# Relative-position attention and a gated FFN: the order of SyncE's scratch transfers, 8 KB rows for queries and keys, and a smaller first block

## The reference, cut to what matters

```python
Q, K, V = (x @ W.T).reshape(b, s, H, HD).transpose(0, 2, 1, 3)      # for each of Wq, Wk, Wv
idx = clip(r[None, :] - r[:, None], -256, 256) + 256
scores = (einsum('bhqd,bhkd->bhqk', Q, K) + einsum('bhqd,qkd->bhqk', Q, pek[idx])) / SCALE
attn = softmax(where(causal, scores, -inf))
out = einsum('bhqk,bhkd->bhqd', attn, V) + einsum('bhqk,qkd->bhqd', attn, pev[idx])
x = layernorm(x + out @ Wo.T)
x = layernorm(x + (silu(x @ wg.T) * (x @ wu.T)) @ wd.T)             # wg, wu, wd = integers / 127
```

## Time and profile before

| | |
|---|---|
| median of 3 runs | 6102.4 us (6099.91 to 6109.79) |
| the profiled execution, whole | 6102.18 us |
| its span in the trace | 6100.5 us |
| busy, share of the span | PE 86%, DVE 63%, ACT 56%, POOL 32% |
| moved by DMA | 1488.37 MB, mean 244 GB/s |

### The profile page before, as it was taken

How to read it: one execution, slowest core, us unless ns; L and a number is a source line. 1 busy time by engine, 2 the same in 40 slices (tenths; PEclk the granted TensorE clock), 3 DMA queues, 4 the chain that set the end, 5 groups by cost and what they waited for, 6 DMA issues and landing times. The chain is left out here.

```text
span 6100.5 us, 143149 instructions
## 1 busy us (share of the span) xinstructions
PE 5228.9 (86%) x49460; PEld 3460.5 (57%) x49460; DVE 3820.3 (63%) x8777; ACT 3442.9 (56%) x7512; POOL 1936.5 (32%) x2580
## 2 busy tenths in 40 slices
PE   9968888888888888888888888888888889999999
PEld 5645555555555555555555555555555546556665
DVE  5646666666666666666667666666666645555554
ACT  4546767667666667767667666766667611111111
POOL 4443333333333333333333333333333311111111
PEclk9989999999999999999999999999999989999999
DMA  8989999999999999999999999999989821121111
GB/s 247 281 228 296 299 290 296 297 292 298 296 289 293 292 297 305 295 295 296 289 300 301 297 293 295 299 292 290 298 276 302 282 77 55 57 64 58 55 55 38
DMA packets 694267, 1488.37 MB, mean 244 GB/s; under 512 B 68132, under 2 KB 365704, under 8 KB 693640
## 3 DMA queue, kind: packets, MB, share of 16 engines
q1 hardware_dynamic: 693640, 1480.16, 76.9%
HBM read 775.21 MB, written 704.65 MB: 243 GB/s over the span
## 5 line engine op out<-in xcount | busy, mean ns | idle before, releaser
L746 ACT ACTIVATE a_prob<-a_neg_s,a_neg_max 128x384 f32<-128x384 f32 (+2 forms) x2048 | 1177.6, 575 | 188.9 <-DVE a_neg_max L795 168.3
L717 PE MATMUL a_t_ps<-a_ident,a_band 128*128 128x128 f32 x3840 | 646.3, 290 | 579.9 <-DMA a_band<-prob_scr 565.3
L478 DVE COPY a_p_t<-a_t_ps 128x512 f32<-128x512 f32 (+3 forms) x1536 | 954.7, 622 | 281.3 <-PE a_t_ps L710 274.4
L753 ACT ACTIVATE a_b_out<-a_t_ps 128x512 f32<-128x512 f32 (+1 forms) x1024 | 583.0, 570 | 904.9 <-PE a_t_ps L653 903.1
L643 PE MATMUL a_s_ps<-a_k,a_q 96*128 96x512 bf16 (+3 forms) x3072 | 880.8, 342 | 140.8 <-ACT a_far L750 127.8
L710 PE MATMUL a_t_ps<-a_ident,a_prob 128*128 128x128 f32 x5376 | 949.1, 279 | 0.4 <-DVE a_band_t L484 0.2
L795 DVE CUSTOM_DVE_ANT_1 a_neg_s<-a_s_ps,a_bias,a_far_neg 128x384 f32<-128x384 f32 x1280 | 791.1, 618 | 237.2 <-DVE a_far_neg L789 237.2
L671 PE MATMUL a_o_ps<-a_p_t,a_v 128*32 128x128 f32 x18432 | 862.9, 303 | 0.2 <-ACT a_o_t L758 0.2
L789 DVE TENSOR_REDUCE a_far_neg<-a_s_ps 128x1 f32<-128x640 f32 (+4 forms) x1280 | 709.9, 555 | 218.1 <-PE a_s_ps L643 165.1
L717 PEld LDWEIGHTS a_t_ps<-a_ident,a_band 128*128 128x128 f32 x3840 | 440.5, 147 | 713.1 <-issue 525.3
L753 ACT ACTIVATE a_p_t<-a_t_ps 128x512 f32<-128x512 f32 (+3 forms) x1536 | 669.1, 436 | 157.8 <-PE a_t_ps L710 152.0
(11 more groups left out here) (97 smaller groups left out, 6551.8 us busy)
## 6 DMA issues: line engine op xcount, KB each, us to landing
a_bias<-bias_scr SPq DMA_DIRECT2D x512, 576.0 KB, 5.5
bias_scr<-a_b_out SPq DMA_DIRECT2D x512, 512.0 KB, 6.6
a_band<-prob_scr SPq DMA_DIRECT2D x512, 512.0 KB, 6.5
prob_scr<-a_prob SPq DMA_DIRECT2D x448, 576.0 KB, 7.2
qk_scr<-p_parts SPq DMA_DIRECT2D x128, 384.0 KB, 3.2
a_q<-qk_scr SPq DMA_DIRECT2D x384, 128.0 KB, 5.2
a_k<-qk_scr SPq DMA_DIRECT2D x384, 128.0 KB, 5.9
prob_scr<-a_wide SPq DMA_DIRECT2D x64, 576.0 KB, 6.6
```

What stands on the lines that cost most here:

```text
L478: copy(p_t[par][:, u, blocks[0] * P:(blocks[-1] + 1) * P], bank[:, 0:len(blocks) * P]) \
L717: mm = pe.transpose(bank[:, n * P:(n + 1) * P], band[:, kk % 2, 2 * i + n // 2, (n % 2) * P:(n % 2 + 1) * P], ident[:, :])
L746: e = act.activation(near_prob(k, u, near(qb)), neg_s[:, u % 2, 0:w].rearrange("p (b c) -> p b c", c=P), ACT.Exp, bias=neg_max[:, u:u + 1] ...
L753: read_out(act, lambda o, i: act.activation(o, i, ACT.Copy), "act", r, k, u, first, last)
```

## The change

Three things, and what they bring with them.

1. On SP the bias write of tile k+3 stands ahead of the bias read of tile k+2; before it stood behind the loads.
2. Queries and keys are stored so that four heads of one feature lie side by side: the columns of Wq and Wk are permuted when ACT copies them (line 190), a row of `qk_scr` for one part and feature holds 4 x 1024 tokens (8 KB), and the terms are put in the orders (0, 1, 2, 0, 1, 0) and (2, 1, 0, 1, 0, 0), so that runs of three, two and one parts can be loaded as one DMA each (`RUNS`): six loads of a group where there were twelve, in steps 0 to 3; v comes in step 4. The key parts are stored in reversed order. The projection writes each m with two DMAs of 64 partitions.
3. In the first query block only the half that exists is moved, packed to rows of 512 elements (`run_of`), both ways; ACT writes its probabilities straight to `wide0`, and POOL has nothing to add there.

The rows of `bias_scr` get a pitch of 1152 elements (`WIDE`) with zero padding behind each, where they had 1024.

```diff
-TERMS_Q = (0, 0, 1, 1, 0, 2)
-TERMS_K = (0, 1, 0, 1, 2, 0)
+TERMS_Q = (0, 1, 2, 0, 1, 0)
+TERMS_K = (2, 1, 0, 1, 0, 0)
+RUNS = ((0, 3, 0), (3, 2, 0), (5, 1, 0)), ((0, 3, 0), (3, 2, 1), (5, 1, 2))
...
-                        sp.dma_start(qk_scr[m // 2, r * 2 + m % 2, :, :, j * CHUNK:(j + 1) * CHUNK]
-                                     .rearrange("s p t -> p s t"), parts[:, m]).then_inc(part_saved[m], 16)
+                        for g in range(2):
+                            sp.dma_start(qk_scr[m // 2, r * 2 + m % 2, g, :, :, j * CHUNK:(j + 1) * CHUNK]
+                                         .rearrange("s p t -> p s t"), parts[g * P // 2:(g + 1) * P // 2, m]) \
+                                .then_inc(part_saved[m], 16)
...
-                act.activation(w_t[:, n // 2, n % 2], tr_ps[:, n % 2, 0:dim], ACT.Copy).then_inc(w_ready, 1)
+                dst, src = w_t[:, n // 2, n % 2], tr_ps[:, n % 2, 0:dim]
+                if n < 4:
+                    dst = dst.rearrange("p (g d h) -> p g h d", d=HD, h=GRP)
+                    src = src.rearrange("p (g h d) -> p g h d", d=HD, h=GRP)
+                act.activation(dst, src, ACT.Copy).then_inc(w_ready, 1)
...
-        LOADS = 2
+        LOADS = ((0, 0),), ((1, 0),), ((0, 1), (0, 2)), ((1, 1), (1, 2))
...
+        def run_of(qb):
+
+            return ROW if qb else GRP * P
...
+            def load_qk(r, g, some=((0, 0), (1, 0), (0, 1), (0, 2), (1, 1), (1, 2))):
+                for which, n in some:
+                    first, count, at = RUNS[which][n]
+                    rows = qk_scr[which, r, g].rearrange("s (d h) t -> (s d) (h t)", h=GRP)
+                    dst = (q_s, k_s)[which][first * HD:(first + count) * HD, g].rearrange("p h t -> p (h t)")
+                    sp.dma_start(dst, rows[at * HD:(at + count) * HD, :]).then_inc(qk_loaded[g], 16)
...
                         sp.wait_ge(p_saved[(k - 2) % 4], quad(r, k - 2))
-                        src = bass.AP(prob_scr.tensor, (k - 2) % 4 * P * WIDE + 1, [[WIDE + 1, P], [1, ROW]])
-                        sp.dma_start(band[:, par].rearrange("p h j -> p (h j)"), src).then_inc(p_loaded[par], 16)
+                        n = run_of(q_block(k - 2))
+                        src = bass.AP(prob_scr.tensor, (k - 2) % 4 * P * WIDE + 1, [[n + P + 1, P], [1, n]])
+                        sp.dma_start(moved_band(k - 2), src).then_inc(p_loaded[par], 16)
...
+                    if ok(k + LEAD):
+                        par = (k + LEAD) % 2
+
+                        sp.wait_ge(b_evac, 2 * TILES * r + 2 * (k + LEAD) + 2)
+                        n = run_of(q_block(k + LEAD))
+                        rows = bias_scr[(k + LEAD) % 4, P:P + P * (n + P)].rearrange("(q c) -> q c", c=n + P)
+                        sp.dma_start(rows[:, 0:n], moved_bias(k + LEAD)).then_inc(b_saved[par], 16)
                     if k + 2 >= 0 and ok(k + 2):
...
                         sp.wait_ge(b_saved[par], pair(r, k + 2))
-                        src = bass.AP(bias_scr.tensor, slot * (P + P * ROW) + P - 1, [[ROW - 1, P], [1, WIDE]])
-                        sp.dma_start(bias[:, par, B_RAW:B_RAW + WIDE], src).then_inc(b_loaded[par], 16)
+                        qb = q_block(k + 2)
+                        n, at = (WIDE, P - 1) if qb else (GRP * P, 2 * P - 1)
+                        src = bass.AP(bias_scr.tensor, slot * (P + P * WIDE) + at, [[run_of(qb) + P - 1, P], [1, n]])
+                        sp.dma_start(bias[:, par, B_RAW:B_RAW + n], src).then_inc(b_loaded[par], 16)
...
-                    if ok(k + LEAD):
-                        par = (k + LEAD) % 2
-
-                        sp.wait_ge(b_evac, 2 * TILES * r + 2 * (k + LEAD) + 2)
-                        rows = bias_scr[(k + LEAD) % 4, P:P + P * ROW].rearrange("(q c) -> q c", c=ROW)
-                        sp.dma_start(rows, b_out[:, par].rearrange("p h j -> p (h j)")).then_inc(b_saved[par], 16)
...
+                if qb == 0:
+                    pool.sem_inc(wide_ready, 1)
+                    return
```

More of the change, by code:

```diff
@@ L204, in middle @@
                         if j or not first:
-                            act.wait_ge(part_saved[m], 16 * (2 * r + j))
-                        act.activation(parts[:, m, 1], rest[:, m % 2], ACT.Copy).then_inc(mid_ready, 1)
+                            act.wait_ge(part_saved[m], 32 * (2 * r + j))
+                        act.activation(part(m, 1), rest[:, m % 2], ACT.Copy).then_inc(mid_ready, 1)
                     for m in range(4):
@@ L229, in _ @@
         def _(dve):
[L230 removed]
+            dve.wait_ge(w_loaded, 16 * 6)
             dve.wait_ge(v_pad, 1)
@@ L243, in body @@
                             dve.wait_ge(lo_ready, n - 1)
-                        dve.tensor_tensor(rest[:, m % 2], full[:, m % 2], parts[:, m, 0], ALU.subtract) \
+                        dve.tensor_tensor(rest[:, m % 2], full[:, m % 2], part(m, 0), ALU.subtract) \
                             .then_inc(rest_ready, 1)
@@ L488, in read_out @@
                         eng.wait_ge(b_saved[par], pair(r, kk - 2))
-                    copy(b_out[:, par, 2 * i:2 * i + 2, j:], by_head).then_inc(b_evac, 1)
+                    half = run_of(q_block(kk)) // 2
+                    dst = moved_bias(kk)[:, i * half:(i + 1) * half].rearrange("p (h j) -> p h j", h=2)
+                    copy(dst, by_head).then_inc(b_evac, 1)
         @block.sync
```

69 lines of the change are left out of this document (40 added, 29 removed).

## The result

The changed kernel takes 5954.0 us (median of 4, 5937.08 to 5957.97) where the kernel before takes 6105.9: a ratio of 0.9752, interval 0.9732 to 0.9773. It is faster by 2.5%, against a forecast of 5590 us and a range that ended at 5880. The direction was right, the size was not, and the time lies outside the range. The profiled run took 5937.08 us with a span of 5935.4.

The account below looks back on a forecast made before the run. It took SyncE's wait for the bias write's landing to bound attention's steps, with PE late next. 1629 us outside attention, 19 fixed and 512 steps of 7.69 us gave 5585, rounded to 5590 us; range 5440 to 5880.

Parts of the forecast that it names:

- The ring: SyncE in attention: bias write, its landing (median 6.6 us), next bias read, next write; its 1777 us wait goes nearly whole.
- it does not do what it says: Rival in attention: SyncE's wait moves to ACT or p_saved, steps stay at 8.7 us; 6100 us, 2%.
- The sum: Whole kernel: 1629 + 19 + 512 x 7.69 = 5585 us, rounded to 5590.
- lower end: Attention step: PE alone at full clock, with 209 us of idle unrelated to the band kept; 7.28 us.
- What remains of the wait for the band: PE in attention: a quarter of today's 1.10 us band wait stays, 0.28 us a step.
- Queries and keys, taken at 0: Attention loads with 8 KB rows: 0.7 us DMA time gained a step, not added because PE is late next.
- First block: Attention's first query block moves 0.14 MB a step less, leaving 2.43 MB for the DMA engines.
- Projection, 4 issues of about 0.4 us: Projection writes in halves: 1.6 us more issuing a chunk, hidden in SyncE's 3.3 us wait; taken as 0.
- The rival of the halves: Projection: writes from 64 partitions run at half of 418 GB/s, 13.2 us a chunk, 61 us more; 5650 us, 12%.
- The DMA rival: Attention: DMA engines bound at today's mean of 294 GB/s, 8.27 us a step; 5880 us, 18%.
- The bias read's cover: Attention: masks are wanted late enough to hide the write ahead of the bias read; taken as 0, of 0 to 640 us.
- 7.41 us for the engines: Attention step: middle of the busiest-engine means, 7.52 us by single steps and 7.30 by pairs.

Follow-up runs that it names:

- order_only: The kernel before with the bias write moved ahead of the bias read and nothing else: 6129.6 us, 1.0021.
- band_before: The changed kernel with the band read taking the slot of the tile before, whose prob write landed a step earlier: 5945.4 us, 0.9727.
- old_rows: The changed kernel with the twelve query and key loads of 2 KB rows and whole projection writes of before: 6050.6 us, 0.9878.
- whole_first: The changed kernel with the first query block moved whole again and widened by POOL: 6027.0 us, 0.9856.
- v_merged: The changed kernel with v written in the projection by four DMAs a chunk instead of eight: 5923.6 us, 0.9685.
- loads_later: The changed kernel with q/k/v loads and output store issued behind the prob write, ahead of SyncE's wait for b_out: 5601.5 us, 0.9157.
- loads_only: The changed kernel with only the q/k/v loads moved behind the prob write, the output store left in place: 5624.1 us, 0.9192.
- band_early: The changed kernel with the band read of tile k-1 issued in step k between bias write and bias read: 6366.3 us, 1.0404.

## Why the prediction was wrong, point by point

- **"So a step can't be shorter than landing of the write, plus the issues between read and write"**: the step that failed. The ring was there, but it was not the only one of that length. 1777 us of waiting at line 543 were taken for 1777 us that go. The row of the same view that would have stopped this was at hand: 380.8 us in 289 steps at line 545, behind the same wait. Where three events end within 0.25 us of each other on the mean, taking one away lets SyncE go on hardly sooner, and the band, for which PE waits, hung on another loop: through `b_out` and the transfers issued behind it. order_only measured what the removal is worth: 1.0021, nothing.
- **The rival "it does not do what it says: the wait moves to the new wait for ACT"** had 2%, at 6100 us. This is what the move did, in order_only to the letter. That the whole change still gained came from parts that the sum held at zero.
- **The sum.** Attention was forecast at 19 + 512 x 7.69 = 3956 us and took 4270, 314 more. 216 of them are PE's wait for the band (359 instead of 0.28 x 512 = 143). The other 98 are the rest of a step, (4270 - 359) / 512 = 7.64 us where the sum had 7.41 and 19 us once: 7.06 of it are PE's busy time and 0.57 its other idle time, 294 us in all, which the prediction's lower end had kept at 209. With the 38 us by which attention starts later, that is 352 us, from the forecast's 5585 to the 5937 of the profiled run; the median lies 17 us above that run.
- **What remains of the wait for the band**: the working found that 13.1 us of landings don't fit in 11.3, and then left a quarter of 1.10 us. The remainder is 359 / 512 = 0.70 us. Discounting the landings as "mostly time in the queue" was the error: the queue was still there, with loads and store in it. The true circle runs through `b_out` and what SyncE issues behind it, not through the prob write (band_before).
- **Queries and keys, taken at 0**: 0.26 us a step, by old_rows. Without them the leg between `b_out` and the band read has 3.4 us instead of 3.0 and the landing 6.4 instead of 6.2: fewer issues there, and perhaps less packet time ahead of the band, which no run took apart. "PE is late next" hid this term.
- **First block**: called room for the DMA engines and not added; 0.14 us a step, by whole_first; its legs are 3.2 and 6.4 us, so it works at the same place.
- **Projection, 4 issues of about 0.4 us in 3.3 us of slack**: mis-sized. Eight halves take 8 x 0.85 = 6.8 us with what stands around each (0.64 of its own and 0.21). Four whole writes at 0.37 and the same 0.21 come to 2.3. That is 4.5 us more, 1.2 over the slack of 3.3, and the chunk grew from 11.3 to 12.4 us. The rival of the halves gave 61 us and 35 came, by another mechanism: SyncE's issues. The rule of the Trainium skill that the rival cited ("SBUF — State Buffer", "Door 1: The DMA port swizzle") would, as the rival read it, have made the chunk longer whatever SyncE issues. v_merged, with writes from 64 partitions still, is back at the chunk of before and at the same 278 GB/s, so here it did not bound the stage; at a DMA share of 0.99 there was little room left.
- **The DMA rival, 5880 us at 294 GB/s**, came nearest in time, with 291 GB/s measured. It is still not the cause: whole_first moved 302 and loads_later 317 GB/s.
- **The bias read's cover** held nearly: DVE's wait for masks rose from 30 to 77 us. **Bias rows of 4608 bytes at 0**: no run took them apart.
- **7.41 us for the engines**: nearly right once the band is in time. loads_later has 7.61 us with 79 us of band waits left, 0.16 a step, so 7.45.
- Of the signs, SyncE's wait at the bias read under 200 us and the new wait for ACT were right, and told nothing about the time. PE's wait for the band (359 us against under 250), 291 GB/s against 316, and 12.4 us a chunk against 11.3 did tell. "PE still waiting over 400 us for the band" as a sign of being wrong missed by its bound.

What stays open: in loads_later, how much comes from SyncE's shorter row of issues (3.0 to 1.8 us) and how much from bytes that are no longer ahead of the band (landing 6.2 to 5.9 us). band_before shows that an earlier issue alone, with the same transfers ahead, brings nothing. The table holds a pair that points at the transfers: band_before and loads_only both issue the band read 2.3 us after `b_out`, but it lands after 6.9 us in the one and 5.7 in the other, and the steps are 8.31 and 7.70 us. It is no clean pair, since the loads moved are also issued elsewhere.

## What to carry to other kernels

Before a wait is removed, look at what ends within a few tenths of it: sum all waits of the queue in that stretch, before and after, and if the sum stays, only the name has changed. Follow the late transfer back through the queue that issues it, and count everything that stands between the event it hangs on and its own issue; move what is in no hurry (loads for later, stores) into the time in which that queue waits anyway. Price a DMA issue in a loop with its surroundings, from one start to the next, and not by its own row. The first of these comes from order_only, the second from loads_later, the third from the projection of this kernel; no other kernel was tried.

## What the hardware showed that was not expected

- In the projection a write of q or k from 64 partitions takes 0.60 us to issue (median of 256; 0.64 at 272.61 above), one from 128 partitions 0.37 in the kernel before (median of 128): half the data, and a longer issue. The two also write to differently shaped rows, and which of the two lengthens the issue wasn't tested.

```profile
259.64 0.37 SPq L106 DMA_DIRECT2D qk_scr<-p_parts  x1
```

- The landing of a read depends on what is ahead of it as much as on itself: the band read of 512 KB took 6.1 us in the kernel after, 6.8 when it was issued 0.6 us earlier, and 3.8 in band_early, where it stands in another place, right behind the bias write:
```profile
a_band<-prob_scr SPq DMA_DIRECT2D x448, 512.0 KB, 3.8
```

- The clock follows the stalls. With PE's band waits at 565, 359 and 79 us the granted clock of attention is 0.95, 0.97 and 0.99, and PE's busy time for the same work (44200 to 44300 instructions) falls with it: 3699, 3616 and 3524 us.
